# A fused two-layer kernel: the seam between the scan, the router and attention put in another order

## The chip, the core and the metric

The program runs on one core of one Trainium2 chip. A core has five engines that run side by side: TensorE (PE, with its weight loads PEld), VectorE (DVE), ScalarE (ACT), GpSimd (POOL) and SyncE (SP, which here only starts transfers). TensorE writes into PSUM, eight banks of 128 partitions by 512 words; everything else lives in SBUF. The metric is the device time of one execution in microseconds. Before the change three executions took 750.39, 750.61 and 751.18 us (median 750.61).

## What is computed

Two layers over x of shape (8, 256, 128), each `x + attn(layernorm(x)) + ffn(layernorm(x))`:

```python
xn = _layernorm(x)
x = x + _L0_attn_ref(xn, ...) + _L0_ffn_ref(xn, ...)   # two Mamba scans (forward, backward); per-sequence top-2 experts
xn = _layernorm(x)
x = x + _L1_attn_ref(xn, ...) + _L1_ffn_ref(xn, ...)   # global, then local attention; top-1 Switch experts with capacity
```

The part that matters here is the second layer's start:

```python
logits = einsum('bnd,de->bne', xn, Wg);  gates = softmax(logits);  mask = one_hot(argmax(gates))
pos = cumsum(mask, axis=1) * mask - mask
dispatch = mask * (pos < 32) * one_hot(pos, 32);  combine = dispatch * gate
expert_inputs = einsum('bnd,bnec->becd', xn, dispatch)
h = gelu(einsum('becd,edh->bech', expert_inputs, W1))
expert_outputs = einsum('bech,ehd->becd', h, W2)
output = einsum('becd,bnec->bnd', expert_outputs, combine)
# attention: q, k = rope(...), then x * rsqrt(mean(x*x) + 1e-6) per head (qk_norm), softmax, values, output projection
```

## The kernel before

The 2048 tokens are 16 tiles of 128. The first layer's scans run over 8 steps (4 blocks of 512 columns, forward and backward) of 16 states, 128 `state` events in all. For each state VectorE runs two scans and one product with C, GpSimd the other product and the drives, ScalarE the decays `exp(dt*A)`, and TensorE turns and adds `hc` into y (`add_y`, L1822) and turns drives (L1800, L1802).

The order is written by hand: `timeline()` returns one list for TensorE and one for the readers (VectorE, ScalarE, GpSimd), and each engine walks its list in order, with semaphores between them. In the last step, norm statistics of the second layer for the first three blocks of rows are laid between states: `("n", k, step)` on ScalarE (`block_norm`: sums L944, mean and squares L948/L952, the scaled rows L957), a power on GpSimd (L702 to L707), then `("xt", k)` turns the block (L1685) and ScalarE copies it (L929), and `("logits", 0)` makes the router's logits of the first 12 tiles (L1697). A scan needs its decay (`decay`, L879), and `drive_turned` where its drive goes over TensorE.

Behind the last state every engine has straight-line code:

- Routing of part 0 (12 tiles): `route_mask`, `gate_y`, `route_pos`, `route_slots` on VectorE (L1464 writes `slot`); TensorE turns the gated y (`turn_y`, L1839) into the one bank `side`, ScalarE copies it (L869), and `finish` (L1848) projects it; VectorE adds it to `x_sb` (L1256).
- The last block's norm (rows 12 to 15): sum, mean, centred rows on VectorE (`norm_part` "A"), squares on ScalarE ("S"), sum and variance on VectorE ("B"), the power -0.5 on GpSimd (L775), the scaled rows on VectorE ("C", L1178), the turn on TensorE ("T", L1677). Then the logits, mask, positions and slots of part 1.
- `spread_slots(k)` (L1968) gathers the expert inputs of two sequences; `turn_slots(n)` (L1977) turns the slots for the combination. The experts can't start before all four `copy_slots`.
- The experts e = 0 to 7: TensorE `up(e)` (L2025) and `down(e)` (L2035), ScalarE four Gelus each (L1086), VectorE copies the output out (L1620). Weights lie in a ring of four; expert e is loaded once `down(e - 4)` is done.
- Between the experts stands the preparation of attention's first two groups, from the list `FILL`, dealt out by `FILL_AT`: `K` and `sqr` (rope, squares and sums of the first group's heads), `inv` (logarithm and exponential on ScalarE, L1039 and L1042, then the product on VectorE, L1567: the inverse root), `split` (values split into two 16-bit parts), `rms`, `T`, `L` of the second group, and `turn` (L2010 for the keys, L2016 for the queries) with VectorE's copies `copy_turned` (L1605, L1607).
- The expert outputs are turned (L2057), and four combination products (L2064) follow, each with VectorE's multiply by the gate (L1625), then one add into `x_sb` (L1629).
- Attention walks `AT_ORDER` and `AT_READERS`: 48 `unit` events (masks L2084, scores L2095, exponentials L1111), `average` (values, L2122), and the preparation of the next groups.

## Time and profile before

| | |
|---|---|
| median of 3 executions | 750.61 us |
| profiled execution, its own time | 749.71 us |
| its span | 747.9 us |
| busy: PE / DVE / ACT / POOL | 639.9 / 581.8 / 530.7 / 416.2 us |
| mean granted TensorE clock | 0.971 of full |

The span is cut into stages: the scans end at about 502 us, the experts run from 525 to 562 us, the combination to 572 us, attention to the end. In a timeline row the bracket at the end names how long the engine was idle before the instruction, and what released it. A granted clock of 1.00 is 2.4 GHz, 0.50 is 1.2 GHz; a mean between them mixes both levels.

### The profile page before, as it was taken

How to read it: one execution, taken by the hardware profiler on the slowest of the kernel's cores; microseconds unless marked ns; L12 is line 12 of the kernel's file. 1: busy time of each engine (PE TensorE's matmuls, PEld its weight loads, DVE VectorE, ACT ScalarE, POOL GpSimd, SP SyncE). 2: the span in 40 equal slices, each digit the busy share in tenths (PEclk: the TensorE clock that was granted, in tenths of full speed). 3: DMA queues.
4: the chain of work that ended last, by engine and by line, in shares of the span. 5: the costliest groups of instructions: out<-in, count | busy, mean ns of one | idle time of the engine just before them, and what ended most of it. 6: DMA issues, size and time to landing. Idle time of an engine off the chain costs nothing.

```text
span 747.9 us, 14099 instructions
## 1 busy us (share of the span) xinstructions
PE 639.9 (86%) x4851; PEld 470.2 (63%) x4851; DVE 581.8 (78%) x847; ACT 530.7 (71%) x1005; POOL 416.2 (56%) x362
## 2 busy tenths in 40 slices
PE   5899987889899798798988985878889989998896
PEld 3488955657667576495776764877767344444443
DVE  7535669999999999999999999996334565666652
ACT  3455475987878969789689899754653778766673
POOL 5400147999999999989999999971000000000000
PEclk8799999999999999999999998999999899999998
DMA  6314558678677797785866868770210000000000
GB/s 208 113 57 124 162 134 218 197 174 264 176 218 234 159 255 184 207 234 153 226 214 168 254 189 204 222 223 0 79 35 1 1 2 1 2 1 2 15 16 29
DMA packets 81414, 100.18 MB, mean 134 GB/s; under 512 B 32560, under 2 KB 37816, under 8 KB 81344
## 3 DMA queue, kind: packets, MB, share of 16 engines
q1 hardware_dynamic: 81344, 99.29, 47.2%
q8 instruction: 39, 0.64, 0.3%
q14 instruction: 31, 0.25, 0.1%
HBM read 96.12 MB, written 3.24 MB: 133 GB/s over the span
## 4 chain that ended last, share of the span: by engine, by line
PE 52%; DVE 17%; issue 14%; ACT 14%; POOL 2%; DMA 0%; DVEq 0%; POOLq 0%; ACTq 0%
PE ps L1822 7%; DVE ps L1204 4%; PE ps L1800 4%; PE ps L2122 3%; DVE hc L1212 3%; PE ps L1873 3%; PE ps L1888 3%; DVE moe L1204 3%; PE ps L1732 2%; PE ps L1816 2%; PE ps L1783 2%; PE ps L1848 2%; PE ps L1752 2%; PE ps L2095 2%; PE ps L2084 2%
## 5 line engine op out<-in xcount | busy, mean ns | idle before, releaser
L683 POOL TENSOR_TENSOR drive<-dtu,b_sb 128x512 f32<-128x512 f32 x160 | 203.2, 1279 | 1.4 <-DMA b_sb<-bc_rows 1.2
L691 POOL TENSOR_TENSOR hc<-moe,c_sb 128x512 f32<-128x512 f32 x128 | 163.3, 1276 | 10.1 <-DVE moe L1204 10.1
L1204 DVE TENSOR_TENSOR_SCAN moe<-ps,drive 128x512 f32<-128x512 f32 x128 | 153.1, 1196 | 0.0
L1822 PE MATMUL ps<-ident,hc 128*128 128x128 f32 x1024 | 137.0, 279 | 0.7 <-POOL hc L691 0.7
L1822 PEld LDWEIGHTS ps<-ident,hc 128*128 128x128 f32 x1024 | 119.5, 145 | 25.5 <-issue 19.9
L879 ACT ACTIVATE ps<-dt,negA 128x510 f32<-128x510 f32 x160 | 106.5, 678 | 28.1 <-DVE moe L1204 27.4
L1204 DVE TENSOR_TENSOR_SCAN ps<-decay_sb,ps 128x512 f32<-128x512 f32 x96 | 117.1, 1220 | 2.1 <-PE ps L1800 1.4
L1111 ACT ACTIVATE probs<-ps 128x1024 f32<-128x1024 f32 (+1 forms) x96 | 86.6, 916 | 36.0 <-PE ps L2095 29.7
L696 POOL TENSOR_TENSOR stat<-stat,halfc 128x4 f32<-128x4 f32 x7 | 7.1, 1008 | 175.7 <-DVE stat L1473 175.7
L1212 DVE TENSOR_TENSOR hc<-ps,c_sb 128x512 f32<-128x512 f32 x128 | 84.9, 664 | 0.0
L879 ACT ACTIVATE decay_sb<-dt,negA 128x510 f32<-128x510 f32 x96 | 68.3, 712 | 15.1 <-DVE ps L1204 15.1
L1800 PE MATMUL ps<-xm,dtuT 128*128 128x128 f32 x384 | 52.3, 279 | 12.1 <-DVE hc L1212 12.0
L910 ACT ACTIVATE scaled<-dtuT,bT 128x128 f32<-128x128 f32 x192 | 60.0, 389 | 0.6 <-PE ps L1802 0.6
L1800 PEld LDWEIGHTS ps<-xm,dtuT 128*128 128x128 f32 x384 | 47.2, 193 | 15.6 <-issue 15.6
L1802 PE MATMUL ps<-ident,scaled 128*128 128x128 f32 x192 | 29.6, 277 | 31.8 <-DVE hc L1212 31.4
L1802 PEld LDWEIGHTS ps<-ident,scaled 128*128 128x128 f32 x192 | 21.2, 141 | 39.3 <-issue 29.5
L2122 PE MATMUL ps<-probs,v_all 128*32 128x256 f32 x640 | 44.5, 397 | 0.0
L1204 DVE TENSOR_TENSOR_SCAN ps<-ps,drive 128x512 f32<-128x512 f32 x32 | 39.1, 1222 | 2.0 <-ACT ps L879 2.0
L769 POOL TENSOR_TENSOR seqstat<-seqstat,halfc 128x2 f32<-128x2 f32 x8 | 5.6, 697 | 58.3 <-DVE seqstat L1402 58.3
L814 ACT ACTIVATE hT<-ps,wbuf 128x256 f32<-128x256 f32 x64 | 25.8, 476 | 16.2 <-PE ps L1873 16.2
L1607 DVE CAST qT<-ps 128x512 f16<-128x512 f32 x32 | 22.1, 689 | 17.4 <-PE ps L2016 17.2
L1888 PEld LDWEIGHTS ps<-wbuf,hT 128*128 128x128 f32 x256 | 30.8, 192 | 3.1 <-issue 2.5
(281 smaller groups left out, 1193.4 us busy)
## 6 DMA issues: line engine op xcount, KB each, us to landing
b_sb<-bc_rows SPq DMA_DIRECT2D x128, 256.0 KB, 4.2
c_sb<-bc_rows SPq DMA_DIRECT2D x128, 256.0 KB, 4.2
xm<-spot_rows SPq DMA_DIRECT2D x48, 256.0 KB, 4.7
wbuf<-in_pack SPq DMA_DIRECT2D x16, 514.0 KB, 3.5
wbuf<-in_pack SPq DMA_DIRECT2D x8, 512.0 KB, 5.7
spot_rows<-c_sb SPq DMA_DIRECT2D x6, 256.0 KB, 4.8
x_sb<-in_x SPq DMA_DIRECT2D x4, 256.0 KB, 3.5
out<-x_sb SPq DMA_DIRECT2D x4, 256.0 KB, 2.3
```

Source lines behind the costliest of these rows:

```text
L683: pool.tensor_tensor(drive_of(N, half), dtu[:, N // STATES % 2, half], b_sb[:, N % B_RING], ALU.mult) \
L691: pool.tensor_tensor(hc[:, 2 * (N % DEEP) + half], h_of(q), c_sb[:, N % C_RING], ALU.mult).then_inc(sem["hc_pooled"], 1)
L879: act.activation(seqs(decay_bank(q))[:, :, lo:lo + SEQ - 1], seqs(dt[:, g % 2, half])[:, :, lo:lo + SEQ - 1], ACT.Exp, scale=negA[:, g // ...
L910: last = act.activation(scaled[:, n % 2, block], dtuT[:, block], ACT.Copy, scale=bT[:, t, j:j + 1])
L1111: act.activation(probs[keys, t % 3, heads_u, 0:width], ps[keys, heads_u, 0:width], ACT.Exp, scale=HD ** -0.5).then_inc(sem["probs_ready"], 1)
L1204: dve.tensor_tensor_scan(h_of(q)[:, turn], decay_bank(q)[:, turn], source[:, turn], 0.0, ALU.mult, ALU.add).then_inc(sem["scan_done"], 1)
L1212: dve.tensor_tensor(hc[:, 2 * (N % DEEP)], h_of(q), c_sb[:, N % C_RING], ALU.mult).then_inc(sem["hc_ready"], 1)
L1800: last = pe.matmul(ps[:, H_BANKS[N % OWN_H], block], dtuT[:, block], spots[:, n % SPOT_RING, block], start=True, stop=True)
L1802: last = pe.transpose(ps[:, H_BANKS[N % OWN_H], block], scaled[:, n % 2, block], ident[:])
L1822: last = pe.matmul(ps[:, Y_BANK + half, block], hc[:, 2 * (N % DEEP) + half, block], ident[:], start=False, stop=True, is_transpose=True, ...
L1888: last = pe.matmul(bank[:, t * D:(t + 1) * D], hT[:, k, c, t * P:(t + 1) * P], wbuf[:, r, HIDDEN + CHUNKS + c * D:HIDDEN + CHUNKS + (c + 1 ...
L2122: last = pe.matmul(to, v, probs[:, t % 3, kv, pair * SEQ:(pair + 1) * SEQ], start=(t % 3 < 2 and pair == 0), stop=(t % 3 != 1 and pair == 1))
```

## The change

Five edits, all between state 120 and the fourth unit of attention. They do the same arithmetic in another order, except that the last block's variance is taken by BN_STATS and BN_AGGR.

1. The last step's `xt 2` and `logits 0` come one state sooner on TensorE, the three parts of `n 2` one state sooner on ScalarE and GpSimd; VectorE reads the logits where it did.
2. The second half of the last y is turned into PSUM bank 2 in place of `side`, and the first group's `T` stands behind both turns.
3. The last block's statistics: four BN_STATS and four BN_AGGR on VectorE in place of two sums, a mean and ScalarE's squares.
4. Routing on TensorE: `spread_slots` 0 and 1, `L`, `T`, one `turn_slots`, the logits, one more, then positions, `spread_slots` 2 and 3, and the other turns of slots later.
5. `inv`, `split` and the turns of the first group leave the expert stage: `inv` stands behind the last expert, `split` behind the first combination product, `turn 0 0` ahead of the last one, `turn 0 1` behind it, `turn 0 2` behind unit 0; the add into `x_sb` stands behind unit 3 on VectorE.

```diff
-            slots.update({9: [("xt", 0)], 11: [("xt", 1)], 14: [("xt", 2)], 15: [("logits", 0)]})
+            slots.update({9: [("xt", 0)], 11: [("xt", 1)], 13: [("xt", 2)], 14: [("logits", 0)]})
...
-                     (7, 10, ("n", 2, 0)), (7, 11, ("n", 2, 1)), (7, 13, ("n", 2, 2))):
+                     (7, 9, ("n", 2, 0)), (7, 10, ("n", 2, 1)), (7, 12, ("n", 2, 2))):
...
-    return tensor_order(order), readers + rest
+    later = [ev for ev in rest if ev != ("logits", 0)]
+    later.insert(later.index(("end",)), ("logits", 0))
+    return tensor_order(order), readers + later
...
-            put(6 * b + at, "turn", b, part)
+            put(6 * b + at + (b == 0 and part == 2), "turn", b, part)
...
+FILL_AT = {e: [] for e in range(1, EXPERTS)}
+FILL_AT.update({1: [("K", 0), ("sqr", 0)], 2: [("rms", 1)], 3: [("T", 1)], 4: [("L", 1)]})
+CLOSE = [("inv", 0), ("split", 0), ("turn", 0, 0), ("turn", 0, 1)]
...
+        LAST_Y_BANK = 2
...
-            for k in range(3):
-                copy_slots(k)
-            norm_part(("T", 2, 3))
-            for n in range(EARLY * 2):
-                copy_slotT(n)
+            copy_slots(0)
+            copy_slots(1)
+            prepare(("L", 0))
+            norm_part(("T", 2, 3))
+            copy_slotT(0)
+            copy_slotT(1)
             route_exp(1)
             act.preload_act_table_set("gelu_apprx_tanh_and_others")
+            copy_slots(2)
             copy_slots(3)
+            copy_slotT(2)
+            copy_slotT(3)
...
             act.preload_act_table_set("natural_log_exp_and_others")
+            prepare(("inv", 0))
...
-            for kind in "ABC":
-                norm_part((kind, 2, 3))
+            for t in range(4):
+                dve.bn_stats(bn6[:, t], x_sb[:, TILES - 4 + t]).then_inc(sem["last_stats"], 1)
+            for t in range(4):
+                dve.wait_ge(sem["last_stats"], t + 1)
+                dve.bn_aggr(bn2[:, t], bn6[:, t]).then_inc(sem["last_aggr"], 1)
+            dve.wait_ge(sem["last_aggr"], 4)
+            dve.tensor_scalar(stat[:, 2, rows], bn2[:, :, 1], LN_EPS, None, ALU.add).then_inc(sem["ln_var"], 1)
+            dve.tensor_tensor(xm[:, rows], x_sb[:, rows], bn2[:, :, 0].unsqueeze(2).broadcast_to([P, 4, D]), ALU.subtract) \
+                .then_inc(sem["ln_centred"], 1)
+            norm_part(("C", 2, 3))
...
+                if k == 0:
+                    prepare(("split", 0))
+                elif k == 2:
+                    copy_turned(0, 0)
+            copy_turned(0, 1)
...
+                elif ev == ("unit", 3):
+                    dve.wait_ge(sem["e_added"], 4)
+                    dve.tensor_tensor(x_sb[:], x_sb[:], sq[:], ALU.add).then_inc(sem["x1_ready"], 1)
...
-            for k in range(3):
-                spread_slots(k)
+            finish(("finish", STEPS - 1))
+            spread_slots(0)
+            spread_slots(1)
+            prepare(("L", 0))
             norm_part(("T", 2, 3))
             turn_slots(0)
+            logits(1)
             turn_slots(1)
-            logits(1)
             prepare(("Q", 0))
             positions(1)
-            for n in range(2, 6):
-                turn_slots(n)
+            spread_slots(2)
             spread_slots(3)
+            turn_slots(2)
+            turn_slots(3)
```

ScalarE's order at states 120 to 122 before. The rows with `decay_sb` or `ps` are decays, `scaled` is a drive, `xnT` the copy of `xt 0`, `sq,stat<-x_sb` the first sums of `n 2`:

```order
L879 ACTIVATE ps<-dt,negA 128x2x255 x2
L910 ACTIVATE scaled<-dtuT,bT 128x128 x4
L929 ACTIVATE xnT<-ps 128x512
L944 ACTIVATE sq,stat<-x_sb 128x128 x4
L879 ACTIVATE decay_sb<-dt,negA 128x2x255
L879 ACTIVATE ps<-dt,negA 128x2x255
L948 ACTIVATE stat<-stat 128x4
L952 ACTIVATE sq,stat<-x_sb,stat 128x128 x4
```

Here both decays of state 121 stand together in the first row, and state 122's stand between the two passes.

ScalarE's order with the change, at the same states:

```order
L885 ACTIVATE ps<-dt,negA 128x2x255
L950 ACTIVATE sq,stat<-x_sb 128x128 x4
L885 ACTIVATE ps<-dt,negA 128x2x255
L916 ACTIVATE scaled<-dtuT,bT 128x128 x4
L935 ACTIVATE xnT<-ps 128x512
L954 ACTIVATE stat<-stat 128x4
L958 ACTIVATE sq,stat<-x_sb,stat 128x128 x4
L885 ACTIVATE decay_sb<-dt,negA 128x2x255
```

The late decay of state 121 (the third row) and everything of `n 2` have changed places, and the second pass has passed state 122's two decays.

TensorE's order from the last y to the router's second logits before (`yg` is the gated y, `xm` the first group, `w_out` the finish, `slot,xn` the gather, `w_g` the logits):

```order
L1952 MATMUL ps<-ident,xm 128x128 x4
L1839 MATMUL ps<-ident,yg 128x128 x8
L1947 MATMUL ps<-xmT,w_kvd 32x512
L1848 MATMUL ps<-w_out,moe 128x128 x8
L1968 MATMUL ps<-slot,xn 128x256 x12
L1677 MATMUL ps<-ident,xn 128x128 x4
L1977 MATMUL ps<-ident,slot 128x128 x8
L1697 MATMUL ps<-w_g,xnT 128x8 x4
L1958 MATMUL ps<-w_q,xmT 128x128 x4
```

`xm` stands ahead of `yg` here, L ahead of the finish, and three quarters of the gather directly behind it.

TensorE's order with the change, at the same place:

```order
L1870 MATMUL ps<-ident,yg 128x128 x8
L1983 MATMUL ps<-ident,xm 128x128 x4
L1879 MATMUL ps<-w_out,moe 128x128 x8
L1999 MATMUL ps<-slot,xn 128x256 x8
L1978 MATMUL ps<-xmT,w_kvd 32x512
L1704 MATMUL ps<-ident,xn 128x128 x4
L2008 MATMUL ps<-ident,slot 128x128 x4
L1724 MATMUL ps<-w_g,xnT 128x8 x4
L2008 MATMUL ps<-ident,slot 128x128 x4
L1989 MATMUL ps<-w_q,xmT 128x128 x4
```

The first group's turn has moved behind y, L behind the gather of two pairs, a turn of slots behind the logits; the third pair's gather has moved behind these rows.

TensorE's order from the turned expert outputs into attention before (`slotT` is the combination, `masks` and `qT,kT` the first unit):

```order
L2057 MATMUL ps<-ident,xe 128x128 x16
L2064 MATMUL ps<-slot,slotT 128x128 x32
L2084 MATMUL ps<-masks,ident 64x512 x4
L2095 MATMUL ps<-qT,kT 128x512 x2
L1958 MATMUL ps<-w_q,xmT 128x128 x4
```

The combination is one run of 32 products, and the scores follow at once; the turns of the first group stand far ahead, between the experts.

TensorE's order with the change, at the same place (`ks` is the key turn, `qs` a query turn):

```order
L2092 MATMUL ps<-ident,xe 128x128 x16
L2101 MATMUL ps<-slot,slotT 128x128 x24
L2042 MATMUL ps<-ident,ks 128x128 x2
L2101 MATMUL ps<-slot,slotT 128x128 x8
L2048 MATMUL ps<-ident,qs 128x128 x4
L2122 MATMUL ps<-masks,ident 64x512 x4
L2133 MATMUL ps<-qT,kT 128x512 x2
L2048 MATMUL ps<-ident,qs 128x128 x4
L1989 MATMUL ps<-w_q,xmT 128x128 x4
```

The key turn has moved in ahead of the last quarter of the combination, the query turns to either side of the first unit.

## Rows read from the trace of the kernel before

**Rows 1.** The page, part 2: granted TensorE clock in 40 equal slices, in tenths
```profile
PEclk8799999999999999999999998999999899999998
```

**Rows 2.** Window of the last scans: busy (x count) of PE, PEld, DVE, ACT, POOL; clock
```profile
480.00:500.00 20.00, 14.48 (x123) 13.49 (x122) 20.00 (x23) 15.65 (x44) 18.59 (x18) 0.99 0.75 221
```

**Rows 3.** Timeline, end of the scan loop: start, length, engine, line, operation [idle <- releaser]
```profile
477.90 0.69 ACT L879 ACTIVATE ps<-dt,negA 128x510 f32<-128x510 f32 x1 [1.77 <-DVE moe L1204]
...
478.37 0.67 DVE L1256 TENSOR_TENSOR x_sb<-acc,ps 128x512 f32<-128x512 f32 x1
...
481.07 0.60 ACT L929 ACTIVATE xnT<-ps 128x512 f32<-128x512 f32 x1 [1.28 <-PE ps L1685]
...
482.74 0.71 ACT L879 ACTIVATE decay_sb<-dt,negA 128x510 f32<-128x510 f32 x1
...
483.96 0.19 ACT L948 ACTIVATE stat<-stat 128x4 f32<-128x4 f32 x1
...
484.62 1.22 DVE L1204 TENSOR_TENSOR_SCAN ps<-decay_sb,ps 128x512 f32<-128x512 f32 x1
...
485.74 0.71 ACT L879 ACTIVATE decay_sb<-dt,negA 128x510 f32<-128x510 f32 x1
```

**Rows 4.** Timeline from the last scan to the first expert product
```profile
504.22 1.29 DVE L1244 TENSOR_TENSOR yg<-ps,z_s 128x512 f32<-128x512 f32 x2 [0.62 <-PE ps L1822]
...
505.90 3.55 DVE L1464 TENSOR_TENSOR slot<-route,iota 128x1536 f32<-128x1536 f32 x2
...
506.42 0.66 PE L1839 MATMUL ps<-ident,yg 128*128 128x128 f32 x4 [0.74 <-ACT moe L869]
...
507.98 2.05 PE L1848 MATMUL ps<-w_out,moe 128*128 128x128 f32 x16
...
510.13 0.69 DVE L1256 TENSOR_TENSOR x_sb<-acc,ps 128x512 f32<-128x512 f32 x1 [0.68 <-PE ps L1848]
...
514.13 1.01 POOL L775 TENSOR_TENSOR stat<-stat,halfc 128x4 f32<-128x4 f32 x1 [11.72 <-DVE stat L1173]
...
525.28 1.99 PE L2025 MATMUL ps<-xe,wbuf 128*128 128x256 f32 x8 [0.98 <-ACT xe L1057]
```

**Rows 5.** Timeline: the nearest small VectorE operations, 4 and 128 columns wide
```profile
511.57 0.17 DVE L1165 TENSOR_SCALAR stat<-stat 128x4 f32<-128x4 f32 x1
...
532.67 0.29 DVE L1543 COPY v_all<-ps 128x128 f32<-128x128 f32 x1 [0.60 <-PE ps L1956]
```

**Rows 6.** Timeline of the expert stage: the waits, and the first transpose behind it
```profile
541.14 0.28 PE L2010 MATMUL ps<-ident,ks 128*128 128x128 f16 x2 [1.40 <-DVE ks L1571]
...
541.59 1.28 ACT L1086 ACT_TABLE_LOAD   x1
...
544.15 1.13 PE L2035 MATMUL ps<-probs,wbuf 128*128 128x256 f32 x4 [0.94 <-ACT probs L1086]
...
547.83 0.38 PE L2016 MATMUL ps<-ident,qs 128*128 128x128 f16 x4 [1.69 <-DVE kT L1605]
...
562.66 1.97 PE L2057 MATMUL ps<-ident,xe 128*128 128x128 f32 x16 [0.52 <-DVE xe L1620]
```

**Rows 7.** Tile wbuf, 528 to 560 us: landing of the last four experts' weights
```profile
DMA to landing us min/median/max: 3.4/3.4/3.5
```

**Rows 8.** Timeline: the start of the attention stage
```profile
571.81 0.69 DVE L1625 TENSOR_TENSOR sq<-ps,rstat 128x512 f32<-128x512 f32 x1 [1.09 <-PE ps L2064]
...
572.05 0.39 PE L2095 MATMUL ps<-qT,kT 32*128 32x512 f16 x2
...
572.54 2.29 DVE L1629 TENSOR_TENSOR x_sb<-x_sb,sq 128x2048 f32<-128x2048 f32 x1
...
576.08 1.10 PE L1956 MATMUL ps<-w_kvu,latT 32*128 32x64 f32 x8 [1.02 <-DVE rot L1535]
...
577.77 1.79 PE L2122 MATMUL ps<-probs,v_all 128*32 128x256 f32 x16
...
583.96 1.07 PE L2122 MATMUL ps<-probs,v_all 128*32 128x256 f32 x16
```

More of the change, by code:

```diff
@@ L1088, in _ @@
                 if e == 0:
-                    copy_slotT(6)
-                    copy_slotT(7)
+                    for n in range(4, 8):
+                        copy_slotT(n)
                 for ev in FILL_AT.get(e, ()):
```

41 lines of the change are left out of this document (25 added, 16 removed).

## The prediction

> **What bounds the kernel now.** I read the slices first [rows 1]: TensorE's clock is full (2.4 GHz) nearly everywhere, with short falls behind the start and in slices 25, 32 and 40, so the change has to be judged by waits, not by the clock. Then the window of the last scans [rows 2]: VectorE is busy 20.00 of 20 us, so each scan is on the path, and ScalarE, 15.65 busy, is only just ahead of it. Then the timeline of the seam, from releaser to releaser. Behind the last scan no engine is full: the path hops from VectorE to TensorE to ScalarE and back, and each hop is a wait that one can price [rows 4]. In the expert stage TensorE is the path, with three idle pieces of its own [rows 6]. At attention's start it waits once for VectorE [rows 8]. The change touches all four places, so the sum goes along the path, place by place, against the profiled execution (749.71 us; the median of the runs shown, 750.61, is 0.90 above, and I carry the difference over). About 0.2% (1.5 us) is what a measurement of this kernel can tell from no change.
>
> **1. The end of the scans.** Logits one state sooner take TensorE's backlog away from the last `hc` turns: VectorE's wait of 0.62 us before `gate_y` goes [rows 4], to within the 0.03 us of a hand-over, so 0.59 is there to be won. Against it stands ScalarE. Its sums of `n 2` now come ahead of the late decay of state 121, but they need the finish of step 6, which ends at 478.37 + 0.67 = 479.04 [rows 3]. Ahead of state 122's first decay then lie the stretch 477.90 to 485.74, less its wait of 1.28 (the time that it used to stand still) and less state 122's two decays (483.96 - 482.74 = 1.22): 5.34 us. So 479.07 + 5.34 + 0.71 for the decay itself = 485.12, where the scan used to start at 484.62: a stall of 0.5 on the full engine. GpSimd's power waits for the same sums and moves its product with C back by some 2 us; the scan that reuses the buffer comes two states later, and I reckon that it is still covered, by half a microsecond. The last drive's turn, now behind the logits, ends near 498.5, where it is wanted at 498.74 + 0.5. Net **-0.1**.
>
> **2. Routing up to the experts.** With y's second half in a bank of its own the wait of 0.74 for ScalarE's copy goes, and `T` no longer stands ahead of y; the finish would start 1 us sooner. But VectorE is in `route_slots` until 505.90 + 3.55 = 509.45, less the 0.1, so its add starts at 509.38 and not at 510.13: 0.75 gained of the 1. The statistics: before, 3.28 us from the end of the add (510.85) to GpSimd's power (514.13). Now four BN_STATS and four BN_AGGR, which no row shows. From below, each costs what the smallest operation does, 0.17; from above, each BN_STATS 0.69, as a whole 512-column operation [rows 4, 5]. I take 0.29 for BN_STATS, by the 128-column row, and 0.17 for BN_AGGR, with 0.20 for the variance: 1.16 + 0.68 + 0.20 = 2.04. Subtraction lies beside the power. So the power starts at 509.38 + 0.72 + 2.04 + 0.08 = 512.2, 1.9 sooner. TensorE meanwhile gathers two pairs and makes L until about 513.95, just when the scaled rows are there. All of part 1's chain moves with it; the last gather ends near 522.3. Before, the fourth copy also sat behind the table load; now the load is over by then, but the two turns of slots behind the gather cover the copy. First expert product at 523.2 in place of 525.28 [rows 4]: **-2.0** more.
>
> By the Trainium skill (VectorE: DVE Perf Modes, "The TRN2 errata — SBUF-src ops pay a fixed extra latency per instruction"), small tiles pay the fixed cost per tile, and it advises 512 elements or more: it speaks against this edit, eight small operations for three. By its formula for fp32 adds, (N+151)/0.96 ns, the eight would be an estimate of 1.82 us against my 1.84 from rows, so it changes nothing unless BN_STATS costs far more than an add.
>
> **3. The expert stage.** `inv` and `split` leave, and with them three table loads of 1.28 us between Gelus. What they are worth is not 3.8 us of ScalarE but TensorE's idle pieces: 1.40 (key turn waits for the split), 0.94 (down of expert 3 waits for Gelus behind the loads), 1.69 (query turn waits for VectorE's copy, held behind the second group's norm) [rows 6]. Sum 4.03. The three turns leave the stage too, about 0.7 by their lengths. Against: the second expert's product now has four slot copies on ScalarE ahead of its Gelus, 0.3 us, and `T` of the second group just meets its norm, 0.1. Net **-4.3**, from 562.66 - 525.28 = 37.4 to 33.1 us. Weights don't take it back: they land 3.4 to 3.5 us after their issue [rows 7], and between `down` of one expert and `up` of the one four later there remain some 8 us.
>
> **4. The combination.** Before, the first scores (572.05) stand directly behind the last product; VectorE's last multiply starts at 571.81 [rows 8]. `inv`'s two activations lie behind the last Gelu, hidden; its product of VectorE lies beside the turns of the outputs. `split` fits beside the second product: the key turn, 0.28, costs 0.15 in the stream. But the query turn needs the key copy, and its own copy has to wait behind VectorE's last multiply: 0.69 for the multiply and 0.69 for the copy (a cast of the same size, taken at the same price), less what the masks cover: the scores come 1.35 later behind the last product than before. **+1.35**.
>
> **5. Attention's start.** The add of 2.29 us stood ahead of the rope of the second group, and `K` on TensorE waited 1.02 for it [rows 8]. Now the add stands behind the key copy, where VectorE was idle before; `K` starts almost at once. The query turn of 0.3 behind unit 0 comes in. From the first scores to the first `average` 572.05 to 577.77 = 5.7 becomes about 4.8: **-0.9**. Behind it the rest of attention keeps its own pace and moves as a block.
>
> The sum: -0.1 - 2.0 - 4.3 + 1.35 - 0.9 = **-6.0 us**: 743.7 by the profile, **744.6** for the median.
>
> The clock is a term that I leave at nothing. The same 16 `average` matmuls took 1.79 us at the lower level and 1.07 at the full one [rows 8], so one fall there costs 0.7; it may go, or come at the new gap ahead of the first scores. Both ends stay in the range.
>
> **The rivals.**
> - BN_STATS is dear: each of the four at 0.69, and BN_AGGR no cheaper than 0.29. Then the power starts 3.28 us - (2.76 + 1.16 + 0.20) = 0.8 later relative to the add, and part 2 gives nothing: 746.7. The rule of the page named above points here. The rows of 128 columns speak against it. 8%.
> - ScalarE's decays come late in more than one state: the margin of GpSimd's product and that of the last drive's turn are each about half a microsecond, and if both fail the scans lose 1 to 2 us more: 746.4. 8%.
> - The add of 2.29 us ahead of the second group's `K` on VectorE lands on the path: its heads are squared behind the fourth exponential, and by my sum both are ready within 0.2 us of each other. If it counts in full, 746.9. 8%.
> - Clock: one or two more falls in the seam, 0.7 to 1.4: 746.0. 10%.
> - The change doesn't do what it says: the expert stage is held by something that the three waits only hid, and keeps its 37 us: 748.9. 3%.
> - **Slower**: TensorE falls to 1.2 GHz within the experts and the combination, which are its densest work, because the new gaps come ahead of them. The price: 1.79 - 1.07 = 0.72 in 1.79, so 0.4 us for each us at the lower level. It cancels 6 us from 15 us on; all 33 us of experts would give about +13, less 6: 757. The slices [rows 1] show full clock there in spite of more idle time than will be left. 3%.
>
> My forecast, all terms within their bounds, takes the remaining 60%.
>
> **How the numbers follow.** The forecast's own band is 742.8 (a fall of the clock less, BN_STATS at 0.17) to 746. The rivals up to 747 are in the range, for 8 in 10 with them trimmed at the low end: 742.6 to 747.4. Faster by over 0.2% (under 749.1): all but the last rival and half of the one ahead of it, with 2% for what I don't see, 0.94. Within 0.2%: 0.03. Slower: 0.03.
>
> **What the changed profile would show.** Right: no wait before the first `gate_y`; one gap of about 0.5 on VectorE before a scan of state 122, the only idle time in the scans; BN_STATS near 0.29; the first expert product 2 us sooner; a single table load between the first Gelu and the last exponential's stage, and no wait of TensorE over 0.5 us in the experts; 33 us from first `up` to the turned outputs; 1.0 to 1.4 us of TensorE waiting ahead of the first scores. Wrong: idle TensorE for the second group's `T` or for weights, several gaps between scans, or ScalarE idle in attention behind a late `K`. The step I trust least is the last: that five microseconds won before attention arrive at its end, since its preparation runs in a rhythm of its own, and a group that comes sooner can wait longer.

## The result, and the profile after

The changed kernel takes **745.55 us** (median of 6 runs, 744.09 to 747.41). The ratio of its runs to those of the kernel before on the same chip is **0.9942, 95% interval [0.9926, 0.9959]**, so it is faster by 0.4 to 0.7%, some 4.4 us (5.1 by the two medians, 750.61 for the kernel before); the forecast was 744.6 (742.6 to 747.4). One of the kernel before's six executions there took 834.81 us and is left out of both. The profiled execution is the changed kernel's fastest: 744.09 us, span 742.3, where the one of before had 749.71 and 747.9. That matters below: it is not a typical one.

TensorE's granted clock in 40 slices, to lay beside [rows 1]: slice 32 is above nine tenths now, the low slices 25 and 40 are where they were. (Slices 1 and 2, far from the change, went from 8 and 7 to 9 and 6.)

```profile
PEclk9699999999999999999999998999999999999998
```

The timeline from the gating to the first expert product, which answers to [rows 4, 5] (start, length, engine, line, operation, wait):

```profile
504.19 1.29 DVE L1254 TENSOR_TENSOR yg<-ps,z_s 128x512 f32<-128x512 f32 x2
...
509.45 0.69 DVE L1266 TENSOR_TENSOR x_sb<-acc,ps 128x512 f32<-128x512 f32 x1
...
510.17 0.87 DVE L1602 BATCH_NORM_STATS2 bn<-x_sb 128x6 f32<-128x128 f32 x4
...
510.96 0.36 DVE L1605 BATCH_NORM_AGGREGATE bn<-bn 128x2 f32<-128x6 f32 x4
...
511.61 1.38 POOL L781 TENSOR_TENSOR stat<-stat,halfc 128x4 f32<-128x4 f32 x1 [8.64 <-DVE stat L1607]
...
514.10 0.66 PE L1704 MATMUL ps<-ident,xn 128*128 128x128 f32 x4
...
523.11 1.11 PE L2057 MATMUL ps<-xe,wbuf 128*128 128x256 f32 x4
```

No wait ahead of the gating; the finish add at 509.45; the power 2.5 us sooner, but 1.38 long where it was 1.01; the first expert product at 523.11 instead of 525.28. The expert stage and the start of attention, which answer to [rows 6, 8]:

```profile
528.80 1.99 PE L2067 MATMUL ps<-probs,wbuf 128*128 128x256 f32 x8 [0.25 <-ACT slotT L1074]
...
553.35 1.28 ACT L1102 ACT_TABLE_LOAD   x1
...
565.92 0.69 DVE L1646 TENSOR_TENSOR sq<-ps,rstat 128x512 f32<-128x512 f32 x1 [0.93 <-PE ps L2101]
566.53 0.68 DVE L1627 CAST qT<-ps 128x512 f16<-128x512 f32 x1
...
567.27 0.39 PE L2133 MATMUL ps<-qT,kT 32*128 32x512 f16 x2 [0.82 <-DVE qT L1627]
...
570.40 1.10 PE L1987 MATMUL ps<-w_kvu,latT 32*128 32x64 f32 x8
...
572.09 1.07 PE L2160 MATMUL ps<-probs,v_all 128*32 128x256 f32 x16
```

Between the first `up` and the turned outputs (556.61) TensorE waits only 0.25 us, for a slot copy, and then 0.52 for the last output copy, as it did before. There is one table load, behind the last Gelu.

Fourteen profiles of this study (before, after, and twelve below) agree on the length of each of the first four stages within 0.02 us where no edit touches it and no fall of the clock lies in it. So parts of 0.3 us can be read from the stages, though the time itself varies by 3 us from run to run. The stages, from VectorE's gating to the first expert product, on to the turn of the outputs, to the first scores, and to the first `average` (us; behind them, the stretch from the finish of step 6 to the gating):

| kernel | routing | experts | combination | start | last scans |
|---|---|---|---|---|---|
| before | 21.06 | 37.38 | 9.39 | 5.72 | 25.85 |
| after | 18.92 | 33.50 | 10.66 | 4.82 | 26.17 |
| after, again | 18.92 | 33.50 | 10.66 | 4.83 | 28.53 |
| old statistics | 20.06 | 33.50 | 10.66 | 4.82 | 27.72 |
| old order | 20.20 | 32.13 | 10.66 | 4.82 | 28.19 |
| old experts | 18.92 | 38.52 | 9.38 | 4.83 | 26.27 |
| old add | 18.92 | 33.51 | 10.66 | 5.68 | 28.04 |
| old scans | 18.93 | 33.50 | 10.66 | 4.83 | 25.68 |
| 4 loads more | 18.92 | 38.88 | 10.67 | 4.82 | 27.76 |
| 2 loads more | 18.92 | 36.22 | 10.66 | 4.82 | 27.74 |
| subtraction first | 18.93 | 33.50 | 10.66 | 4.82 | 27.52 |
| sooner turns | 18.92 | 33.50 | 9.83 | 4.82 | 27.70 |
| filled waits | 18.57 | 33.53 | 9.82 | 4.83 | 27.26 |
| one pass | 19.06 | 33.07 | 9.83 | 4.82 | 27.85 |

Behind attention's start nothing takes the gain back by itself: from one group's head norms to the next, before and after both need 22.0 to 22.8, 21.7, 21.2 and 20.9 us, and five groups in a row come 7.07 us sooner (against a kernel before that lost 1.4 to the clock there, see below). In the first profile a fall of the clock at 695 us took 1.5 of it back.

### The profile page after: what moved, and what is told of

The parts are those of the page before. It is cut to its first block, busy times and chain, and to the rows that moved or that the text cites. A ratio compares the mean times of both kernels' runs of the same rounds, so it can differ in the third digit from the quotient of the medians.

```text
span 742.3 us, 14099 instructions
## 1 busy us (share of the span) xinstructions
PE 639.4 (86%) x4851; PEld 468.8 (63%) x4851; DVE 581.2 (78%) x852; ACT 526.4 (71%) x1001; POOL 418.6 (56%) x362
## 4 chain that ended last, share of the span: by engine, by line
PE 50%; DVE 17%; issue 14%; ACT 13%; POOL 4%; DMA 0%; POOLq 0%; DVEq 0%; ACTq 0%
PE ps L1849 5%; DVE hc L1222 4%; DVE ps L1214 4%; PE ps L1827 3%; DVE moe L1214 3%; PE ps L2160 3%; PE ps L1904 3%; PE ps L1919 3%; PE ps L1759 2%; PE ps L1810 2%; PE ps L2133 2%; PE ps L2057 2%; PE ps L2067 2%; PE ps L1779 2%; POOL drive L689 2%
## 5 line engine op out<-in xcount | busy, mean ns | idle before, releaser
L697 POOL TENSOR_TENSOR hc<-moe,c_sb 128x512 f32<-128x512 f32 x128 | 166.1, 1298 | 8.2 <-DVE moe L1214 8.2
L1849 PE MATMUL ps<-ident,hc 128*128 128x128 f32 x1024 | 134.9, 275 | 3.3 <-POOL hc L697 3.0
L1849 PEld LDWEIGHTS ps<-ident,hc 128*128 128x128 f32 x1024 | 116.6, 142 | 28.6 <-issue 19.3
L1829 PE MATMUL ps<-ident,scaled 128*128 128x128 f32 x192 | 30.1, 280 | 27.9 <-DVE hc L1222 27.9
L1829 PEld LDWEIGHTS ps<-ident,scaled 128*128 128x128 f32 x192 | 21.9, 144 | 35.3 <-issue 26.2
```

Source lines behind the costliest of these rows:

```text
L697: pool.tensor_tensor(hc[:, 2 * (N % DEEP) + half], h_of(q), c_sb[:, N % C_RING], ALU.mult).then_inc(sem["hc_pooled"], 1)
L1829: last = pe.transpose(ps[:, H_BANKS[N % OWN_H], block], scaled[:, n % 2, block], ident[:])
L1849: last = pe.matmul(ps[:, Y_BANK + half, block], hc[:, 2 * (N % DEEP) + half, block], ident[:], start=False, stop=True, is_transpose=True, ...
```

## The experiments

Their times are medians, with the ratio to the kernel before on the same chip. Each edit is made to the changed kernel, unless said otherwise.

**The changed kernel again.** No edit.

> The changed kernel unchanged, timed beside the variants of it that undo one part each, and profiled once more. Waits: the gain over the kernel before is 5.9 us again, and every milestone between the last scans and the sixth group of attention stands within 0.1 us of the first profile, counted from the first expert product, except where a fall of TensorE's clock lies in between. Rival, the clock explains it: the milestones scatter by more than 1 us and the gain is not the same. The fall near 695 us that took 1.5 us back in the first profile: if it belongs to the new schedule it comes again at the same place; if it is chance it comes elsewhere and the shift at the end is near 7 us.

744.72 us, 0.9935 [0.9915, 0.9955]. The stages came out the same to 0.01 us and the fall at 695 did not come again (the last head norms at 706.92, those before at 686.00: 20.9 apart, as in the kernel before). By the expectation that makes it chance, but the later profiles say less: the same interval is 22.4 long again in those with the old experts, two loads more and the sooner turns, and the interval ahead of it in the one with the subtraction first. So 5 of the 13 profiles of changed kernels lose these 1.5 us near one place. The one profile of before does not; whether it does so less often is open. And one milestone was off by 2.4 us, a thing that no theory had expected. TensorE and VectorE at the end of the scans in this profile:

```profile
495.10 3.30 PE L1724 MATMUL ps<-w_g,xnT 128*128 128x8 f32 x24
498.26 1.95 PE L1849 MATMUL ps<-ident,hc 128*128 128x128 f32 x8
500.00 1.06 PE L1829 MATMUL ps<-ident,scaled 128*128 128x128 f32 x4
...
501.16 1.23 DVE L1214 TENSOR_TENSOR_SCAN ps<-decay_sb,ps 128x512 f32<-128x512 f32 x1 [2.38 <-PE ps L1829]
```

and in the first profile of after:

```profile
495.06 2.74 PE L1724 MATMUL ps<-w_g,xnT 128*128 128x8 f32 x24
497.66 1.07 PE L1849 MATMUL ps<-ident,hc 128*128 128x128 f32 x8
498.57 0.60 PE L1829 MATMUL ps<-ident,scaled 128*128 128x128 f32 x4
...
498.56 0.67 DVE L1222 TENSOR_TENSOR hc<-ps,c_sb 128x512 f32<-128x512 f32 x1
499.27 1.23 DVE L1214 TENSOR_TENSOR_SCAN ps<-decay_sb,ps 128x512 f32<-128x512 f32 x1
```

L1829 is the turn of the last drive, which the change put behind the logits (L1724). The windows of the repeat (length, TensorE busy, clock, DMA share, GB/s) say why they were slow:

```profile
494.00:496.00 2.00, 1.88 (x17) 1.00 0.90 133
496.00:498.00 2.00, 2.00 (x17) 0.83 1.04 155
498.00:500.00 2.00, 2.00 (x11) 0.50 0.98 384
500.00:502.00 2.00, 2.00 (x11) 0.50 1.04 424
```

The clock is at the lower of its two levels (1.2 GHz) from 497.3 on, though TensorE had been busy. The forecast gave the late turn half a microsecond of margin. Even the first profile, whose clock is full from 494 on, has none left: the turn ends at 499.17, and the scan starts 0.71 behind the product ahead of it, where 0.58 is usual. TensorE had not stood still since 490.90, within an earlier fall of the clock (490.5 to 493.8). With the second fall, in the repeat, the scan waited 2.38 us.

**The last scans as before.**

```diff
-            slots.update({... 13: [("xt", 2)], 14: [("logits", 0)]})
+            slots.update({... 14: [("xt", 2)], 15: [("logits", 0)]})
...
-                     (7, 9, ("n", 2, 0)), (7, 10, ("n", 2, 1)), (7, 12, ("n", 2, 2))):
+                     (7, 10, ("n", 2, 0)), (7, 11, ("n", 2, 1)), (7, 13, ("n", 2, 2))):
...
-    later = [ev for ev in rest if ev != ("logits", 0)]
-    later.insert(later.index(("end",)), ("logits", 0))
-    return tensor_order(order), readers + later
+    return tensor_order(order), readers + rest
```

> The changed kernel with the last step's events as before: the turn of the scaled rows, the logits and the norm of block 2 one state later, and the logits read inside the last step. Waits: the piece of 0.6 us ahead of the gating is back and the 0.35 and 0.19 ahead of the scans of states 122 and 123 are gone, so counted from the scan of state 110 the gating starts within 0.2 us of the changed kernel; the time is the same. Rival, the sooner logits are the gain: 0.6 us above the changed kernel. Rival, the late decay costs more than it gives: up to 0.5 us below.

743.64 us, 0.9932 [0.9909, 0.9956], against 0.9935 and 0.9942 of the changed kernel: the times can't tell them apart. The stretch can: 25.68 us. Over all profiles with the new order of the last step it is 26.17 and 26.27 where the clock does not fall behind 496 us (2 of 12), and 27.26 to 28.53, middle 27.75, where it does (10 of 12), each time with a wait of 1.36 to 2.38 us for the turn of the last drive. With the old order it is 25.68 without such a fall and 25.85 with one (the kernel before: clock 0.50 at 500 to 502, and only its 0.62 ahead of the gating). So this part of the change loses: 0.3 to 0.5 us at best, some 1.9 mostly.

By the stretch, 0.49 shorter than the changed kernel's at its best, the second rival (up to 0.5 us below) holds. And the expectation failed in a way that matters more: with the old order back, the 0.62 us ahead of the gating did not come back. TensorE's windows of the kernel before and of this run (length, busy, clock, DMA share, GB/s), and this run's gating, idle 0.04 us before:

```profile
500.00:502.00 2.00, 2.00 (x12) 0.50 0.97 391
...
500.00:502.00 2.00, 2.00 (x20) 1.00 1.03 422
...
504.79 1.29 DVE L1252 TENSOR_TENSOR yg<-ps,z_s 128x512 f32<-128x512 f32 x2
```

With the logits in the same place, and the clock full, there is no wait. The 0.62 came with the fall of the clock in that one execution (499.5 to 502.9), which is too short to show in [rows 1] or in the 0.99 of [rows 2]. The 0.35 ahead of state 122 is gone with the old order, as expected, but a wait of 0.30 for GpSimd's `hc` (ahead of the scan at 492.52) stands in place of the 0.19, so nothing shows that one to be the new order's. That the new order also makes the fall behind 496 more frequent is suggested by 10 of 12 against 1 of 2, and not shown.

**The statistics as before.**

```diff
-            for t in range(4):
-                dve.bn_stats(bn6[:, t], x_sb[:, TILES - 4 + t]).then_inc(sem["last_stats"], 1)
...
+            norm_part(("A", 2, 3))
+            norm_part(("B", 2, 3))
             norm_part(("C", 2, 3))
```

with the square put back on ScalarE behind `T` of the first group.

> The changed kernel with the statistics of the last block made as before (sum, mean, subtraction, square on ScalarE, sum, variance) and all else new. Waits: the power starts 509.45 + 0.72 + 3.28 = 513.4 instead of 511.6, the scaled rows are there at 515.2 instead of 513.7, and since the turn of them stood at 514.1 the chain and the first expert product come 1.1 us later; the time is 1.1 us above the changed kernel. Rival, the order on TensorE alone made the 2 us of routing: nothing, first expert product at the same place. Rival, the statistics made all of it: 2 us.

746.20 us, 0.9955 [0.9935, 0.9975]; routing 20.06, so 1.14 us longer, and nothing else moved. The forecast of the waits holds; both rivals fall.

**The order of routing as before**, on TensorE and ScalarE, and y's second half in the side bank:

```diff
             positions(0)
-            turn_y(("y", STEPS - 1, 0))
-            turn_y(("y", STEPS - 1, 1))
             prepare(("T", 0))
+            turn_y(("y", STEPS - 1, 0))
+            turn_y(("y", STEPS - 1, 1))
+            prepare(("L", 0))
             finish(("finish", STEPS - 1))
-            spread_slots(0)
-            spread_slots(1)
-            prepare(("L", 0))
+            for k in range(3):
+                spread_slots(k)
             norm_part(("T", 2, 3))
             turn_slots(0)
...
```

> The changed kernel with TensorE's and ScalarE's order of routing as before and the last y in the side bank, but the new statistics kept. Waits: the finish add comes 0.7 later, but the turn of the scaled rows now stands behind three gathers that end near 515.7, whenever the rows are ready; so the shorter statistics are worth nothing here, the first expert product is at 525.1, and the time is 2.0 us above the changed kernel. Rival, the two parts simply add: 2.0 less the 1.1 of the statistics, 0.9 us.

744.46 us, 0.9927 [0.9903, 0.9951]: no loss at all. Both theories were wrong. Routing got 1.28 us longer, and the experts 1.37 shorter. The rows of TensorE:

```profile
511.33 5.35 PE L1993 MATMUL ps<-slot,xn 128*128 128x256 f32 x24
516.51 0.60 PE L1701 MATMUL ps<-ident,xn 128*128 128x128 f32 x4
...
525.87 1.99 PE L2050 MATMUL ps<-xe,wbuf 128*128 128x256 f32 x8 [0.98 <-ACT xe L1063]
```

The turn of the scaled rows does stand behind three gathers, as expected. But the old order has six turns of slots ahead of the first product and two among the experts; the new one four and four. Two turns of slots that used to lie in waits of routing now lie in a stage where TensorE has no waits (in after, L2008 at 527.52, and `down` 1.28 us later at 528.80). The new order wins 1.28 and pays 1.37.

**The first group's inverse root, split and two turns between the experts, as before** (the third turn stays behind unit 0):

```diff
-FILL_AT.update({1: [("K", 0), ("sqr", 0)], 2: [("rms", 1)], 3: [("T", 1)], 4: [("L", 1)]})
+LATER = FILL[4:]
+FILL_AT = {e: LATER[2 * (e - 1):2 * e if e < EXPERTS - 1 else None] for e in range(1, EXPERTS)}
```

> The changed kernel with the inverse root, the split and the first two turns of attention put back between the experts, as before (the third turn stays behind unit 0, and the add into x_sb stays late). Waits: TensorE's three idle pieces are back (1.4, 0.9, 1.7), the experts take 37.2 us instead of 33.5 from the first product to the turn of the outputs, the combination gives 1.3 back, and the time is 2.4 us above the changed kernel. Rival, TensorE's clock or the weights hold the experts: 34 us at most and a time 1 us below the changed kernel.

748.94 us, 0.9993 [0.9976, 1.0011]. This part is nearly the whole gain. The experts took 38.52, the combination 9.38: 3.74 together, where I had expected 2.4. TensorE's waits are those of [rows 6], to the hundredth:

```profile
541.41 0.29 PE L2032 MATMUL ps<-ident,ks 128*128 128x128 f16 x2 [1.40 <-DVE ks L1577]
...
544.41 1.99 PE L2057 MATMUL ps<-probs,wbuf 128*128 128x256 f32 x8 [0.94 <-ACT probs L1092]
...
548.09 0.38 PE L2038 MATMUL ps<-ident,qs 128*128 128x128 f16 x4 [1.68 <-DVE kT L1621]
```

They sum to 4.02 and the stage pays 5.02. A group of `down` starts 1.73 us after the one ahead when nothing waits, though its row is 1.89 long: its end is put later than where the next one could begin. So each wait shown costs about 0.16 to 0.21 more than the row says (three waits, 0.5), the two turns add 0.12 and 0.22, and the group behind the second wait is 0.1 longer (1.99 in place of 1.89).

**Table loads alone.** Four, and then two, behind the square of the heads:

```diff
                 for ev in FILL_AT.get(e, ()):
                     if ev[0] != "turn":
                         prepare(ev)
+                if e == 1:
+                    for n in range(2):
+                        act.preload_act_table_set("natural_log_exp_and_others")
+                        act.preload_act_table_set("gelu_apprx_tanh_and_others")
```

> The changed kernel with four more table loads on ScalarE (5.1 us, to the set of the exponential and back, twice) behind the square of the heads, ahead of the third expert's Gelus; nothing is computed differently. Waits: those Gelus started at 534.16 and TensorE wants the first of them at 537.04; with 5.1 us more the first is ready near 539.6, so TensorE waits 2.5 us in one piece, the experts take 36.0 us instead of 33.5, and the time is 2.5 us above the changed kernel. Rival, ScalarE's time counts in full: 5.1 us more. Rival, the loads were never what held TensorE: nothing.

> As the run with four more table loads, with two of them (2.57 us instead of 5.15). There the third expert's down waited 3.49 us for all four Gelus, so 1.66 us of the loads were hidden. Waits: TensorE waits 0.9 us in one piece, the clock does not fall behind it, and the experts take 34.4 us. Rival, the fall of the clock to 0.68 in that stretch of the run with four comes with any wait here: 35 us or more. Rival, the whole 2.57 counts: 36.1 us.

Four: 751.04 us, 1.0020 [1.0001, 1.0039]; experts 5.38 longer. The rows and windows of TensorE:

```profile
541.89 3.63 PE L2071 MATMUL ps<-probs,wbuf 128*128 128x256 f32 x8 [3.49 <-ACT probs L1094]
...
539.00:542.00 3.00, 0.11 (x1) 0.97 0.08 33
542.00:545.00 3.00, 3.00 (x7) 0.50 0.00 0
```

The number looks like the rival (5.1, all of it), but the rows say otherwise: 3.49 us of waiting, a microsecond more than I had reckoned because `down` waits for all four Gelus and not for its first, and then a fall of the clock right behind that wait, in which the product took 3.63 us, where behind a wait without a fall it took 1.99. Two (one run, 749.46 us; its loads are hidden by 1.66 us):

```profile
540.74 1.99 PE L2070 MATMUL ps<-probs,wbuf 128*128 128x256 f32 x8 [0.91 <-ACT probs L1094]
...
544.08 0.63 PE L1986 MATMUL ps<-ident,xm 128*128 128x128 f32 x4 [1.35 <-DVE xm L1492]
```

The 0.91 came as foretold and no fall behind it. The stage still got 2.72 longer, not 0.9, so the rival (the whole 2.57 counts) had the number, by a path of its own: the loads also delay the second group's square, and with it the norm for which TensorE's next turn waits 1.35 us. A delay on ScalarE has two customers here, and I had followed one.

**The add into `x_sb` ahead of attention, as before.**

```diff
             copy_turned(0, 1)
+            dve.wait_ge(sem["e_added"], 4)
+            dve.tensor_tensor(x_sb[:], x_sb[:], sq[:], ALU.add).then_inc(sem["x1_ready"], 1)
...
-                elif ev == ("unit", 3):
-                    dve.wait_ge(sem["e_added"], 4)
-                    dve.tensor_tensor(x_sb[:], x_sb[:], sq[:], ALU.add).then_inc(sem["x1_ready"], 1)
```

> The changed kernel with the add of all rows into x_sb put back directly behind the query copy, ahead of attention's first events on VectorE, all else new. Waits: the second group's queries wait for it, and the keys on TensorE behind them; from the first scores to the first average 5.7 us instead of 4.82, and all of attention 0.9 us later; the time is 0.9 us above the changed kernel. Rival, the shorter start belonged to the missing fall of the clock (the first average took 1.07 us instead of 1.79): the stretch stays within 0.1 of 4.82, and the time is unchanged. Rival, the add is as much in the way where it now stands: unchanged, or shorter.

746.35 us, 0.9945 [0.9925, 0.9965]. Attention's start 5.68 instead of 4.82, with the first `average` at the full clock: 0.86 us belong to the add's place, none of it to the clock.

**Sooner turns in the combination.**

```diff
-                if k == 3:
-                    turn(0, 0)
+                if k == 1:
+                    turn(0, 0)
+                elif k == 3:
+                    turn(0, 1)
                 pe.wait_ge(sem["e_turned"], k + 1)
...
-            turn(0, 1)
```

and on VectorE the keys' half of the split ahead of the first multiply, the key copy behind the first and the query copy behind the third.

> The changed kernel with the turns of the combination sooner: the keys' half of the split ahead of VectorE's first multiply, the key turn ahead of the second product and the query turn ahead of the last one, each with its copy behind the multiply before. Waits: the copy of the queries no longer stands behind the last multiply, the first scores follow the last product as closely as in the kernel before, at 566.2 to 566.6 instead of 567.27; the time is 0.7 to 1.0 us below the changed kernel. Rival: the last multiply, now behind that copy, or the sums into banks of the scores hold the start as long: nothing.

744.76 us, 0.9928 [0.9909, 0.9948]; combination 9.83 instead of 10.66, 0.83 won back of the 1.27 that the change had given up there. The last multiply no longer stands ahead of the query copy (VectorE):

```profile
567.37 0.68 DVE L1627 CAST qT<-ps 128x512 f16<-128x512 f32 x1
568.82 0.69 DVE L1649 TENSOR_TENSOR sq<-ps,rstat 128x512 f32<-128x512 f32 x1 [0.78 <-PE ps L2108]
```

**Filled waits in routing**, on top of the sooner turns: `T` ahead of y, `L` ahead of the finish, turns of slots ahead of the turn of the scaled rows and ahead of the second positions.

```diff
             positions(0)
+            prepare(("T", 0))
             turn_y(("y", STEPS - 1, 0))
             turn_y(("y", STEPS - 1, 1))
-            prepare(("T", 0))
+            prepare(("L", 0))
             finish(("finish", STEPS - 1))
             spread_slots(0)
             spread_slots(1)
-            prepare(("L", 0))
-            norm_part(("T", 2, 3))
             turn_slots(0)
+            norm_part(("T", 2, 3))
+            turn_slots(1)
             logits(1)
...
```

> The kernel of the sooner turns, and another order of routing: the first group's turn and latents in the waits for y, two turns of slots in the waits for the scaled rows and for the mask. Since the run with the old order showed that the new order only moved turns of slots from waits of routing into the experts, the sum of TensorE's waits decides: three pieces (0.57, 0.30, 0.4 ahead of the turn of the scaled rows) are filled, so the outputs are turned 1.0 us sooner after the gating than in the changed kernel, and together with the combination the time is 1.8 us below it. Rival, ScalarE's copies in this order hold the first product (as 0.98 us did in the run with the old order): 0.8 us below, from the combination alone.

745.16 us, 0.9932 [0.9913, 0.9952]. Routing 18.57, 0.35 shorter and not 1.0; the rest as with the sooner turns. Behind the power the path is a chain (rows, logits, mask, positions, slots, gather, copy), so the turns only moved into its waits; the one that mattered was `L` ahead of the turn of the scaled rows (in the changed kernel the rows end at 513.71, and their turn starts behind `L` at 514.10). The rival is half right: the first product waits 0.25 for ScalarE's copy.

**The subtraction ahead of the variance**, and **one pass for the scaled rows**:

```diff
-            dve.tensor_scalar(stat[:, 2, rows], bn2[:, :, 1], LN_EPS, None, ALU.add).then_inc(sem["ln_var"], 1)
             dve.tensor_tensor(xm[:, rows], x_sb[:, rows], bn2[:, :, 0].unsqueeze(2).broadcast_to([P, 4, D]), ALU.subtract) \
                 .then_inc(sem["ln_centred"], 1)
+            dve.tensor_scalar(stat[:, 2, rows], bn2[:, :, 1], LN_EPS, None, ALU.add).then_inc(sem["ln_var"], 1)
```

> The changed kernel with the subtraction of the mean ahead of the small operation that makes the variance, so that VectorE stands still while GpSimd raises to the power. The power took 1.38 us beside the subtraction and 1.01 us beside an idle VectorE in the kernel before. If the two disturb each other it takes 1.01 again, and the scaled rows come 0.3 us later (0.68 later start, 0.37 shorter). If the length has another cause it stays 1.38, and the rows come 0.7 us later.

```diff
-            dve.tensor_tensor(xm[:, rows], x_sb[:, rows], bn2[:, :, 0].unsqueeze(2).broadcast_to([P, 4, D]), ALU.subtract) \
-                .then_inc(sem["ln_centred"], 1)
-            norm_part(("C", 2, 3))
+            dve.wait_ge(sem["ln_pow"], STAGE["B"]["B", 2, 3] + 1)
+            for t in range(4):
+                k = TILES - 4 + t
+                ins = dve.tensor_scalar(xn[:, k], x_sb[:, k], bn2[:, t, 0:1], stat[:, 3, k:k + 1], ALU.subtract, ALU.mult)
+            ins.then_inc(sem["ln_done"], 1)
```

This second diff stands on top of the filled waits and the sooner turns, and one more turn of slots stands ahead of the first expert product (not shown).

> The kernel with the sooner turns of the combination and the filled waits of routing, with two edits more: the last block is scaled by four operations of one pass each (minus mean, times the root) behind the power, which no longer runs beside a subtraction; and one more turn of slots stands in the wait for the last copy of routing (0.25 us idle there) instead of in the experts. Waits: the scaled rows come 0.2 us sooner, the first expert product 0.5 us sooner after the gating than in the changed kernel, the experts take 33.1 us, and with the 0.83 of the combination the time is 1.8 us below the changed kernel. Rival, the four small operations cost 0.29 each and the power keeps its 1.38: the rows come 0.5 us later, and the time is 1.2 us below it.

With the subtraction first (one run, 745.30 us) GpSimd's row is 1.01 long again; the scaled rows start 0.24 us later after the gating, the turn of them no later (it waits for `L` anyway):

```profile
513.38 1.01 POOL L781 TENSOR_TENSOR stat<-stat,halfc 128x4 f32<-128x4 f32 x1 [9.24 <-DVE stat L1609]
```

The one-pass kernel, 743.68 us, 0.9939 [0.9918, 0.9960], has the short power too, and four operations that together take longer than the two that they replace (0.68 and 0.69). Its timeline, and the view of line L1612 alone (duration in ns, min/median/max):

```profile
514.59 0.96 POOL L782 MEMSET v_all<- 128x1040 f32 x1
...
514.68 1.53 DVE L1612 TENSOR_SCALAR xn<-x_sb,bn,stat 128x128 f32<-128x128 f32 x4 [1.12 <-POOL stat L781]
...
L1612 DVE TENSOR_SCALAR xn<-x_sb,bn,stat x4: 327/550/959, 514.7 to 515.9; 128x128 f32<-128x128 f32 x4
```

1.53 us in place of 0.69 behind the power. But the four are not alike: the first two took 0.96 and 0.77, beside GpSimd's clearing of `v_all` (514.59 to 515.55), the last two, behind it, 0.33 each, 0.25 from start to start. At that pace all four would take 1.08, an estimate from these rows. In the changed kernel the one `tensor_tensor` beside the same clearing took its usual 0.69. No run moves the clearing away, so that it is the cause is read from the overlap and not shown. The turn of slots put in the wait for the last copy did what it should: experts 33.07, 0.43 less. By its stages the kernel is 1.12 below the changed one, near the rival's 1.2, though not for its reasons: the power was short and the four operations dearer than it said. All three better kernels lie within each other's intervals and within the changed kernel's. By the stages alone the best would be the filled waits with that one turn moved and the old order of the last scans: 0.35 + 0.43 + 0.83, and the scans' 1.9 mostly. That combination was not run.

## Why the prediction was right, and where it was not

The measured median lies in the forecast's range, and the sign was right (-6.0 forecast; -4.4, between 3.1 and 5.6, by the ratio on the same chip, -5.1 between the medians, -5.6 between the spans of the profiled executions). The mechanism of the largest part, the experts, is shown. That the total came so near is in part luck: the scans were 2.0 worse and the experts 0.4 worse than forecast, and 1.4 of that was paid by falls of the clock that the sum had left at nothing.

**1. The end of the scans, -0.1.** The gating stood at 504.19 instead of 504.22 in the first profile, but that start carries what came before the stretch; the stretch itself is 0.3 longer there, and 1.9 longer mostly (ten of twelve profiles). Right were the stall ahead of state 122 (0.35 where I had reckoned 0.5) and little else; 0.19 more went for an `hc` that I had taken as covered. Two steps failed. One is "VectorE's wait of 0.62 us before `gate_y` goes ..., so 0.59 is there to be won": I put that wait down to the place of the logits, and the run with the old order has 0.04 there at the full clock. By these two profiles it belonged to a fall of the clock, and at the full clock there was nothing to win against the stall. The other is "the last drive's turn ... ends near 498.5, where it is wanted at 498.74 + 0.5". It ended at 499.17 in the first profile, with no margin, and with a fall behind 496 its scan waited 1.36 to 2.38. The rival on the clock priced a fall in the seam by attention's `average`, 0.7; behind the late turn it costs twice to three times that. The rival with this place and "1 to 2 us more" had it right at 8% and 746.4; the medians, 745.55 and 744.72, lie between it and the forecast.

**2. Routing, -2.0.** Measured -2.14, the first product at 523.11 for 523.2. The four BN_STATS took 0.87 and the four BN_AGGR 0.36, so the power started at 511.61 and not 512.2. The lengths that I had taken for single ones were right, 0.29 and 0.17; adding them end to end was not:

```profile
L1602 DVE BATCH_NORM_STATS2 bn<-x_sb x4: 275/276/295, 510.2 to 510.8; 128x6 f32<-128x128 f32 x4
L1605 DVE BATCH_NORM_AGGREGATE bn<-bn x4: 147/148/164, 511.0 to 511.2; 128x2 f32<-128x6 f32 x4
```

One is 0.28 us long and the next starts 0.20 behind it; of BN_AGGR, 0.15 and 0.07. The 0.6 us more that this gained was then lost to a power of 1.38 us beside the subtraction and to `L`, which held the turn of the scaled rows. By itself the part on statistics is worth 1.14 with the new order, and the order nothing: I counted what it won before the experts and not the two turns that it sent there. As for the Trainium skill's rule on small tiles (VectorE: DVE Perf Modes, "The TRN2 errata — SBUF-src ops pay a fixed extra latency per instruction"): for BN_STATS and BN_AGGR the trace bears out the formula for a single one (0.28 to 0.30, and 0.15 to 0.16), but not the sum: eight of them took 1.15 us where the estimate by the formula was 1.82. For the one-pass kernel's four `tensor_scalar` the rule speaks in the right direction: 512 columns in four took 1.53 us, and would take 1.08 by the undisturbed ones, against 0.69 in one.

**3. The experts, -4.3.** Measured -3.88. The mechanism holds: with the old place the waits are back to the hundredth. Two terms of the sum were mis-sized. The removed waits and turns are worth 5.02 to 5.25 (from before to the run with the old order, 37.38 to 32.13), not 4.7: each wait costs 0.2 more than its row shows. The cost against them was 1.4, not 0.4: the two more turns of slots, for which the sum had only ScalarE's copies. No wait of TensorE among the experts names the weights. One price in the rivals was also wrong, in the one called slower: 0.4 us is the cost of each us spent at the lower level, but the 33 us of experts are their length at the full clock. At 1.79 to 1.07 they would take 55, so 22 more and not 13, and a time near 767; that did not come about in any run.

**4. The combination, +1.35.** Measured +1.27. The run with sooner turns wins 0.83 of it back, so so much was the query copy's place behind the last multiply; the rest is about the two turns in TensorE's stream (0.11 and 0.32 from their starts to what follows). TensorE waited 0.82 ahead of the first scores, less than the 1.0 to 1.4 foretold, and the query turn's 0.32 in the stream, which the sum did not have, made up for it.

**5. Attention's start, -0.9.** Measured -0.90, and 0.86 with the add alone put back. The gain arrived at the end: the step I trusted least was sound.

**The clock, left at nothing.** In the kernel before, the two falls at attention's start (578 to 581, 588 to 592) cost 1.4 us (from the start of the first `average` to the first head norms it took 4.60 us, all others 3.44, and the next group lost another 0.24). None of the thirteen profiles of changed kernels has the first, the one with the old experts and the one with the old add included; a single fall in the second's place, at 582 to 585, stands in two (filled waits, one pass) and cost 0.1. What keeps them away is open, and with a single profile of before so is how often they come there. The sum of what the stages show is -2.14 - 3.88 + 1.27 - 0.90 + 1.9 - 1.4 = -5.2 us. Its last two terms are differences to that single profile, and the fall of 1.5 us near the last groups, in 5 of 13 profiles, is not in it.

## What to carry to other kernels

When work is reordered on the engine that bounds the next stage, add up that engine's work and waits over both stages: an order that starts the next stage sooner with work left over has won nothing. A reckoned margin of half a microsecond on an engine whose clock can halve is no margin; keep what the full engine waits for ahead of work that can be late. And where runs scatter by 3 us, take stage lengths between fixed milestones of the trace: they agreed to 0.02 us and told apart edits that the medians of five to twelve executions could not. Before a wait in a single profile is put down to the order of the work, look at the clock in narrow windows: a fall of 3 us does not show in a slice of 19.

## What the runs showed of the hardware

- BATCH_NORM_STATS2 on 128x128 fp32 took 0.28 us and started every 0.20, BATCH_NORM_AGGREGATE on six values 0.15 and every 0.07: four tiles of 128x128 had their means and variances in 1.15 us.
- A `tensor_scalar` of 128x128 fp32 with two operands per partition took 0.33 us and started every 0.25, but 0.96 and 0.77 beside a clearing by GpSimd (one profile, one pass); a `tensor_tensor` of four times the columns took 0.69, beside the same clearing too.
- GpSimd's power on 128x4 took 1.38 us in the ten profiles in which VectorE's subtraction of 128x512 overlapped its first 0.51, and 1.01 us in the four kernels in which VectorE stood still (before, old statistics, subtraction first, one pass). It is not any work of VectorE that stretches it: beside the scans it took 1.01 too (at 488.07 in the kernel before).
- TensorE's clock fell right behind a wait of 3.49 us in its densest stage, and not behind waits of 0.91, 1.40 or 1.69 there. But in the repeat it also fell at 497.3 us, in a stretch where TensorE was busy 2.00 of 2 us, 3.4 us after the fall before had ended.
- Four table loads in a row took 5.15 us, 1.28 each, with 0.01 between them.
